# A two-layer graph network on one core: gathered rows of 128 bytes and four copies made by TensorE, in place of rows of 512 bytes that hold the copies

## The reference

```python
# layer 0: edge network, maximum over incoming edges
e_feat = concatenate([x[src], x[dst], edge_attr])
v = relu(e_feat @ W1 + b1) @ W2 + b2
h = layernorm(x + maximum(segment_max(v, dst), x))

# layer 1: relation-aware messages with a gate per edge
xs, yd = h[src], h[dst]
msg = einsum('eb,ebo->eo', w_comp[etype], einsum('ei,bio->ebo', xs, weight))   # 16 bases
a = tanh(relu(sum((xs @ A1.T + A1_b) * (yd @ A2.T + A2_b + rel_emb[etype])) / sqrt(32)))
nei = segment_sum(a * msg, dst)
out = layernorm(h + relu(where(in_deg > 0, nei + h[src[last_e]] @ self_loop_weight, 0)))
```

## Time and profile before

| | |
|---|---|
| median of 3 runs | 4698.58 us (4695.1 to 4704.23) |
| profiled execution | 4697.75 us, its span 4696.0 us |
| mean granted clock of TensorE | 0.874 |
| busy shares: PE, PEld, DVE, ACT, POOL | 76%, 35%, 56%, 20%, 75% |
| DMA packets, bytes | 387141, 448.88 MB |

### The profile page before, as it was taken

One profiled execution on the slowest core, in us unless ns is written; L12 is line 12 of the kernel. 1 busy time (PEld: TensorE's weight loads), 2 busy tenths in 40 slices (PEclk: granted clock), 3 DMA queues, 4 the chain that ended last, 5 costly groups with the idle time before them and its releaser, 6 DMA issues.

```text
span 4696.0 us, 62687 instructions
## 1 busy us (share of the span) xinstructions
PE 3559.1 (76%) x18080; PEld 1650.3 (35%) x18279; DVE 2630.5 (56%) x3543; ACT 924.9 (20%) x1615; POOL 3502.1 (75%) x3530
## 2 busy tenths in 40 slices
PE   5639999998999999981047777777777777777751
PEld 2315555544444444441013333233333333323321
DVE  5624444434434333434137777777777777777754
ACT  3401111111111111110012222222222222222211
POOL 7777777777777777767777777777777777777755
PEclk8869999999999999995568888988888888888875
DMA  8123333322222222223134454454454454445521
GB/s 312 28 58 79 79 75 78 78 71 69 69 71 68 67 70 70 69 55 64 33 91 121 126 121 119 124 125 115 123 125 120 118 124 126 119 121 125 120 67 33
DMA packets 387141, 448.88 MB, mean 96 GB/s; under 512 B 165171, under 2 KB 288976, under 8 KB 384752
## 3 DMA queue, kind: packets, MB, share of 16 engines
q1 hardware_dynamic: 241968, 197.51, 18.8%
q0 software_dynamic: 112832, 141.36, 13.0%
q10 hardware_dynamic: 32256, 109.07, 6.0%
HBM read 324.74 MB, written 122.85 MB: 95 GB/s over the span
## 4 chain that ended last, share of the span: by engine, by line
DMA 32%; issue 12%; POOL 5%; PE 1%; DVE 0%; POOLq 0%; ACT 0%; DVEq 0%; ACTq 0%
DMA xg<-h_dram,src_idx 30%; POOL xg L541 4%; DMA last_rows<-sum_rows,last_i 2%; DVE late L994 0%; PE psum L1193 0%; PE psum L1184 0%; POOL last_rows L541 0%; PE psum L1235 0%; POOLq L536 0%; DVE scan L1009 0%; DMA sum_rows<-early 0%; PE psum L1170 0%; PE psum L1242 0%; POOLq L362 0%; PE psum L1099 0%
## 5 line engine op out<-in xcount | busy, mean ns | idle before, releaser
L541 POOL DMA_INDIRECT xg<-h_dram,src_idx x1664 | 1603.6, 964 | 536.1 <-DMA xg<-h_dram,src_idx 471.1
L541 POOL DMA_INDIRECT xg<-in_x_dram,src_idx x1468 | 1514.6, 1032 | 457.8 <-DMA xg<-in_x_dram,src_idx 413.5
L994 DVE TENSOR_TENSOR late<-late,psum 128x512 f32<-128x512 f32 x1664 | 1107.0, 683 | 547.8 <-PE psum L1184 523.8
L1113 PE MATMUL psum<-late 128*128 128x448 bf16 x4116 | 862.1, 363 | 0.0
L1235 PE MATMUL psum<-ident,xg 128*128 128x128 f32 x1664 | 332.2, 336 | 462.9 <-DMA xg<-h_dram,src_idx 455.5
L1184 PE MATMUL psum<-comp,sel 128*128 128x512 bf16 x1482 | 590.9, 419 | 8.6 <-DVE late L994 4.0
L1113 PEld LDWEIGHTS psum<-late 128*128 128x128 bf16 x4116 | 411.3, 101 | 465.2 <-issue 154.8
L922 DVE TENSOR_TENSOR_SCAN scan<-fresh,scan,psum 128x512 f32<-128x512 bf16 x103 | 131.8, 1280 | 762.8 <-PE psum L1151 762.8
L1193 PE MATMUL psum<-late,basis 128*32 128x512 f32 x3328 | 515.2, 696 | 4.3 <-DVE late L994 0.8
L1235 PEld LDWEIGHTS psum<-ident,xg 128*128 128x128 f32 x1664 | 259.9, 176 | 535.0 <-issue 471.2
L686 ACT COPY late<-psum 128x512 f32<-128x512 f32 x416 | 243.9, 586 | 853.4 <-PE psum L1235 806.5
(11 more groups left out here) (137 smaller groups left out, 3505.9 us busy)
## 6 DMA issues: line engine op xcount, KB each, us to landing
sp_in<-spread SPq DMA_DIRECT2D x208, 256.0 KB
late<-type_dram SPq DMA_DIRECT2D x104, 512.0 KB, 8.4
sum_rows<-early ACTq DMA_DIRECT2D x104, 512.0 KB
spread<-late ACTq DMA_DIRECT2D x16, 1664.0 KB, 38.2
ea<-in_edge_t SPq DMA_DIRECT2D x104, 256.0 KB, 2.7
keep<-keep_dram SPq DMA_DIRECT2D x832, 32.0 KB
max_rows<-out ACTq DMA_DIRECT2D x104, 256.0 KB, 2.0
xg<-h_dram,src_idx POOLq DMA_INDIRECT x1664
```

The source lines that it names most:

```text
L541: pool.indirect_dma_start(out=out, out_offset=None, in_=table, in_offset=bass.IndirectOffsetOnAxis(ap=index, axis=0), engine_sem=pool_issu ...
L994: dve.tensor_tensor(prod[:, n % G_BUFS, :], x4[:, s.slot(2), g, :], bank[C_BANK[n]][:, :], ALU.mult).then_inc(prod_ready, 1)
L1113: last_ = pe.matmul(bank[8 - HOT + tile][:, 0:PICK * F], class_hot[:, s.slot(2), c, P * tile:P * tile + P], x_parts[:, c, q, :], start=c = ...
```

## The change

`h_dram` holds each row of h once, 128 bytes. SP writes each chunk of h once. The gathers of layer 1 fetch rows of 128 bytes, as many calls as before. The tile of layer 1 is no longer one of its own size: `xg` is the first two slots of `xg0`. In `source_turn`, each transpose is replaced by four products of the gathered 128x32 block (as the weights, at column position 32b) with the identity (as the moving operand); each writes one group of 32 partitions of the bank. ACT's copy reads the whole row.

```diff
-        h_dram = dram("h_dram", [NODES, 4 * F])
+        h_dram = dram("h_dram", [NODES, F])
...
-        xg = sb("xg", [P, 2, SLOTS, 4 * F])
-        xg0 = xg[:, :, :, :].rearrange("p a k (b f) -> p (a k b f)", f=F).rearrange(
-            "p (u k f) -> p u k f", u=PRE, f=F)
+        xg0 = sb("xg0", [P, PRE, SLOTS, F])
+        xg = xg0[:, 0:2, :, :]
...
-        h_nodes = h_dram.rearrange("(p t) (c f) -> p t c f", p=P, f=F)
+        h_nodes = h_dram.rearrange("(p t) f -> p t f", p=P)
...
-                for k in range(4):
-                    sp.dma_start(h_nodes[:, cols, k, :], h[:, cols, :]).then_inc(h_out, 16)
+                sp.dma_start(h_nodes[:, cols, :], h[:, cols, :]).then_inc(h_out, 16)
...
-            pool.wait_ge(h_out, 4 * 16 * CHUNKS)
+            pool.wait_ge(h_out, 16 * CHUNKS)
...
-                act.copy(out1[:, s.slot(4), :, F:2 * F], xg[:, s.slot(2), :, 0:F]).then_inc(src_copied, 1)
+                act.copy(out1[:, s.slot(4), :, F:2 * F], xg[:, s.slot(2), :, :]).then_inc(src_copied, 1)
...
                 for j in range(TILES):
-                    last_ = pe.transpose(out[:, j, :], xg[:, s.slot(2), j * STREAMS + g, :], ident[:, :])
+                    for b in range(4):
+                        last_ = pe.matmul(out[F * b:F * b + F, j, :], xg[:, s.slot(2), j * STREAMS + g, :],
+                                          ident[:, :], start=True, stop=True, tile_position=(0, F * b))
                 last_.then_inc(x_turned[1], 1)
```

## The result

| | kernel before | changed kernel |
|---|---|---|
| median of 9 runs each, us | 4704.22 (4695.1 to 4713.58) | 4720.47 (4712.25 to 4728.56) |
| profiled execution, us | 4697.75 (span 4696.0) | 4723.29 (span 4721.5) |
| ratio | | 1.0034, 95% interval 1.002 to 1.0047 |

The change makes the kernel 16 us slower. The prediction was 4700.6 us with a range up to 4716, so the time lies 4 us above the range, on the slower side, which was given a chance of 0.15.

A forecast was written before the change was run, and what follows sets the result against it. Layer 1 was taken to run at the pace at which POOL issues gathers. The last step's turns add 2 us, all else 0, to the profiled execution's 4697.75 us; with 0.8 us to the median: 4700.6 us, range 4668 to 4716.

The forecast's parts named there:

- What bounds the kernel: Layer 1 runs at the pace at which POOL issues gathers, 20.53 us per step, with nothing left over.
- The gathers: Layer 1's gathers: POOL's price of a call does not hang on the row size, so 0 us.
- The products: PE's source_turn: products in place of transposes add 2.6 to 3.6 us per step, covered by PE's wait, so 0 us.
- about 1.25 us: Length expected of one PE turn on line 1235 after the change, in place of 0.60 us.
- The tail: Last step's turns, which no gather follows: 2 us onto the path, with 0 and 3.6 us as bounds.
- Between the layers: SP's fewer writes of h, the tile as a view and ACT's dense source copy: 0 us.
- the term of 0.29 us per step for longer calls: Part of POOL's step in layer 1: calls' mean of 963 ns over the median of 945, 16 x 18 ns.
- PE's cover: PE's 4.34 us wait per step for the gather's landing, before the first turn, said to hide the longer turns.
- rival 3: Other losses: longer POOL calls where DVE work moves under them, or the larger PE loop; 4712 to 4800 us, chance 0.05.
- Rival 1: Layer 1's long POOL gaps belong to the 512-byte rows, so 25 us go: 4676 us, chance 0.24.
- Rival 2: In source_turn, weight loads wait for the wave before, so PE's turns outlast the gap: about 4850 us, chance 0.09.
- serial case: PE's products in source_turn run wholly one after another, 4.3 us per turn: about 5500 us, chance 0.01.

The follow-up runs named there:

- m_after_no_hold: Changed kernel with index loads two steps ahead, sum_scan reading weigh's product from PSUM, build_hot as seven tensor_scalar instructions: 4569.25 us, ratio 0.973.

## Why the prediction was wrong

- What bounds the kernel: right. Layer 1 is POOL's sum before and after, 16 x 1.25 us, long calls and gaps; 2080 / 1608 calls x 16 = 20.70 us per step against 20.53.
- The gathers cost POOL the same whatever the row: right, 938/945 ns again, and 954 against 955 ns on the mean once the scan holds no call.
- The products: right. A turn of 32 records takes 1.08 us at the upper clock (granted 1.00), eight waves of 0.135 us, and 1.94 us at the lower (granted 0.50); "about 1.25 us" lay between. PE's wait is 172.9 / 101 = 1.7 us per step, granted clock 0.93, and the price uncovered is 3.1 us per step.
- The tail: 2 us taken, 1.1 us in the changed kernel and 1.9 us in m_after_no_hold.
- Between the layers: right. From the last call of layer 0 to the first of layer 1 it is 273.3 us before and 272.9 after.
- **The step that failed is the term of 0.29 us per step for longer calls.** It was read off as 16 x 18 ns, taken as a constant of POOL, and the price of PE's longer turns was set to 0 because PE's wait covers them. What was not asked is which DVE instruction makes a call long and where in POOL's period it lies. PE's cover hid the work from POOL's waits, but moved all of DVE behind it. The term measured 16 x 29 ns = 0.46 us, 17.5 us over the stage. The mechanism stood in rival 3, with "nothing points to one" and a chance of 0.05; the time lies at the lower end of its 4712 to 4800. One look at the ends of the 34 calls over 1.2 us would have shown the scan.
- Rival 1 (the long gaps go with the 512-byte rows): wrong. Gaps without a releaser are still there in the changed kernel, 115 waits of 59.9 us in place of 59.7.
- Rival 2 (turns outlast the gap): wrong where POOL is the bound. Where it is not, layer 1 is 3.1 us per step longer, within the 2.6 to 3.6 us that the products were priced at; 32 records in 1.08 us show that its mechanism, a load that waits for the wave before, does not act. Its serial case does not give the 5500 us named: 4 x 3.88 us less the 4.34 us of cover, 103 times, is about 5850 us, and about 5390 us with the second reserve of 4.5 us.

The Trainium skill has the rule that decides here, on the page "SBUF — State Buffer", section "SBUF: two separate sides": DVE and GpSimd share a pair of SBUF ports under an exclusive lock, which a DVE instruction takes in a two-port mode or, against a GpSimd instruction that reads SBUF, with two inputs in SBUF. With this the trace agrees: 40 and 71 held calls, and none behind the scan once one input is in PSUM. Which of the two cases one_hot falls under, no run here shows. For a DVE instruction in a two-port mode the page's part "A bandwidth-pool intuition that's wrong (but worth ruling out)" gives its end and about 0.115 us as the end of the hold; some rows behind one_hot have 0.12 us, others 0.82 us, and those behind the scan have 0.75 us, so here the measurement decides. The same skill's page "Runtime: NRT & Kernel Launch", section "Instruction fetch mechanics", says that a taken branch to a target outside the two pages of code at hand waits until that code is fetched. The trace has such waits for a PE loop of 1790 instructions, 4.4 us at each return (100.0 us in 23 waits), and none for one of some 890; where between the two the limit lies, no run shows.

## What to carry to other kernels

When one engine issues all the time and a group's mean stands above its median, list its long instructions and what ended just before each of them: that excess is a price that depends on the phase between two engines, and any edit that moves the other engine moves it, even if the edit is covered. Better than to keep a lucky phase is to remove the hold: where DVE ran beside gathers issued by POOL, moving one of two SBUF inputs to PSUM ended the hold of the scan. One SBUF input alone is no guarantee, as one_hot shows, so look for held calls again after the edit. The cover of a step says that its time is hidden, not that what comes behind it stays where it was.

## What the runs showed of the hardware

- A gather issued by POOL is held by sum_scan, a DVE instruction with two SBUF inputs, if the scan started 0.1 us or more ahead of the call and runs over the point 0.2 us after the call's start. The call then ends 0.75 us after the scan; behind build_hot it is 0.82 us. PSUM as one input of the scan removes the hold. Such holds cost 116 us of layer 0 (behind build_hot) and, by its phase, 15 to 45 us of layer 1 (behind the scan).
- one_hot, with one tensor input in SBUF (bf16, 128x2048), holds calls as well: they end 0.12 us or 0.82 us after it.
- 32 products of 128x32 blocks with 128 columns in four column groups take 1.08 us at the upper clock and 1.94 us at the lower, four transposes of 128x128 take 0.60 us.
- A PE loop body of some 1770 to 1790 instructions is fetched again at each return, with a stand of about 4.4 us (the body of 1790); bodies of some 900 are not.
- There are executions in which some of PE's matmuls signal up to 11 us after their end, while PE stands, and the same kernel takes 6766 to 6793 us in place of 4700.
